# Summing both scan directions inside the forward units of a bidirectional Mamba kernel, against summing them in the output stage

## The chip, the cores and the metric

The kernel runs on one core of one Trainium2 chip. The metric is the device time of one execution in microseconds (us); lower is better. All data is float32.

## The reference, cut to what matters

An image of 1024 channels by 64 x 64 pixels is normalised, goes through a short decaying scan over channels and a token norm (stages that the change does not touch), and then through a bidirectional Mamba block over 4096 tokens:

```python
xz = (hidden @ in_proj_w.T).transpose(0, 2, 1)      # 2048 channels of x, 2048 of z
x, z = jnp.split(xz, 2, axis=1)
y_fwd = _direction(x, ...)                          # conv of 4 taps, projections, selective scan, 16 states
y_bwd = _direction(x[:, :, ::-1], ...)[:, ::-1, :]
y = (y_fwd + y_bwd) * silu(z.transpose(0, 2, 1))
out = nan_to_num(y @ out_proj_w.T)                  # then the residual is added
```

## The kernel before, in words

**Layout.** Tokens are cut into 8 chunks of 512 (`NCH`, `T`), the 2048 inner channels into 16 blocks of 128 (`DB`, `P`). A *unit* is one block of one chunk in one direction: 256 units (`NU`), first the 128 backward ones (chunks from the last to the first), then the 128 forward ones (`HALF` = 128). The kernel is a row of stages, with all engines joined between them; two matter here.

**`stage_scan`.** Every engine has its own program; semaphores join them. The order inside a unit is written out by hand over n = 0 to 15, the scan's states. For each n ScalarE (ACT) makes the decay `da` (L1026) and saves the end state of an earlier n (`save`, L1006); VectorE (DVE) scans (L1169) and, for 12 of the 16 states, multiplies with C (L1179, `weigh`); GpSimd (POOL) makes the scan's input `w` (L1120) and the products of the other four (L1129). TensorE (PE) adds all products of a unit up by transposing them one over the other into the bank `yT` (L893, L918, L926), so a unit's result is held by tokens, 128 tokens on partitions and 128 channels along the row. `yT_copy` (L987 to L992) moves it to `y_out` at n = 2 of the next unit, and the DMA queue of SyncE (SP) stores it (L742) to the scratch `yT` of its direction, one contiguous tile of 128 x 512 for each unit. The very last one is stored by L803.

PE also makes z: `in_step` in two halves at n = 0 and 2 of a forward unit, into the bank `in_ps`, which `in_copy` (L969 to L973) empties at n = 7 into `z_out`, two buffers; L768 stores it by channels to the scratch `z`, 2048 x 4096. Backward units make the next x the same way. The x projection of a chunk adds 16 blocks up in `proj_ps`, opened and closed by a matmul with zeros (`open_projection`, `close_projection`, L833 to L838). Before the units stand eight rounds of `before_scan`, on PE and ACT as a hardware loop (L936, L1079).

SP's program for a unit (L728 to L778) is in order: loads of the next-but-one unit's `wdt` and `xc`, the store of `y_out`, the broadcasts of B and C in the last unit of a chunk and the first of the next, the stores of `xc` and `z`, then at L770 a wait for **all** stores so far (`stored_to`), and behind it the loads of x, `wx` and `win` for later units.

**`stage_out`.** For each chunk 16 blocks are prepared and 8 groups of 128 output channels are made. To prepare a block, SP loads three tiles (L1263, L1265, L1267: forward y, backward y, z) into one of four slots, POOL adds the two y (L1293), PE transposes the sum in four 128 x 128 pieces (L1315), ACT makes silu(z) (L1303) and DVE multiplies the two into `yg` (L1343). A group is 16 float32 matmuls of 128 x 512 (L1325), which the profile shows as 32 (each is done in two passes), into one of two banks. DVE copies, cleans up and adds the residual (L1354 to L1366), SP stores. `chunks` (L1232) interleaves: at step q of chunk c an engine first prepares two blocks of chunk c + 1 and then does group q of chunk c; SP prepares one step ahead. Chunk 0 has nothing to hide behind. The eight 1 MB loads of `wout` stand on SP's queue behind chunk 0's tiles (L1268 to L1270), and chunk 1's first tiles behind them.

## Time and profile before

| what | us |
|---|---|
| median of 3 runs | 8527.85 (8518.41 to 8528.65) |
| the profiled execution, its own time | 8523.32 |
| its span, first to last instruction | 8521.3 |
| output stage, first DMA issue to the end of the span | 7484.4 to 8521.3, 1036.9 |
| PE busy, DVE busy, POOL busy, ACT busy | 7199.0, 7468.1, 6869.8, 4922.4 |

Times in rows are microseconds from the span's start. In a timeline row the first number is the start, the second the duration, then engine, line of the kernel, operation, and what it writes and reads; in brackets stands how long the engine had been idle and what ended the wait. PEld are weight loads of PE, SPq is SP issuing a DMA. A busy PE is not PE at its peak, since the ends of matmuls are modelled.

### The profile page before, as it was taken

How to read it: one execution, taken by the hardware profiler on the slowest of the kernel's cores; microseconds unless marked ns; L12 is line 12 of the kernel's file. 1: busy time of each engine (PE TensorE's matmuls, PEld its weight loads, DVE VectorE, ACT ScalarE, POOL GpSimd, SP SyncE). 2: the span in 40 equal slices, each digit the busy share in tenths (PEclk: the TensorE clock that was granted, in tenths of full speed). 3: DMA queues.
4: the chain of work that ended last, by engine and by line, in shares of the span. 5: the costliest groups of instructions: out<-in, count | busy, mean ns of one | idle time of the engine just before them, and what ended most of it. 6: DMA issues, size and time to landing. Idle time of an engine off the chain costs nothing. (4 is left out here: it accounts for less than half of the span.)

```text
span 8521.3 us, 107499 instructions
## 1 busy us (share of the span) xinstructions
PE 7199.0 (84%) x28624; PEld 4125.5 (48%) x28624; DVE 7468.1 (88%) x8300; ACT 4922.4 (58%) x11720; POOL 6869.8 (81%) x3058
## 2 busy tenths in 40 slices
PE   7568888888888888876888888888888887779999
PEld 3243554555555555544455545455554545434444
DVE  6922999999999999999999999999999999934443
ACT  3743666666666666666666666666666666610000
POOL 0613999999999999999999999999999999921110
PEclk9789999999999999977899999999999998889999
DMA  3273131323131323121223232323232322153442
GB/s 84 74 203 129 64 114 64 113 67 113 63 114 64 113 67 114 64 96 43 103 73 125 73 127 74 122 73 125 74 127 74 123 74 105 46 187 133 139 139 78
DMA packets 540787, 843.35 MB, mean 99 GB/s; under 512 B 112576, under 2 KB 260032, under 8 KB 522816
## 3 DMA queue, kind: packets, MB, share of 16 engines
q1 hardware_dynamic: 540224, 837.03, 29.6%
q8 instruction: 208, 3.41, 0.2%
q14 instruction: 355, 2.91, 0.1%
HBM read 583.83 MB, written 253.02 MB: 98 GB/s over the span
## 5 line engine op out<-in xcount | busy, mean ns | idle before, releaser
L1120 POOL TENSOR_TENSOR scan_w<-scan_du,scan_bcast_b 128x2048 f32<-128x2048 f32 x1023 | 4629.7, 4536 | 3.6 <-DMA scan_bcast_b<-bc 3.6
L1169 DVE TENSOR_TENSOR_SCAN scan_h<-scan_da,scan_state,scan_w 128x512 f32<-128x512 f32 x3072 | 3766.3, 1269 | 21.9 <-issue 14.5
L926 PE MATMUL scan_yT<-all_ident,scan_hc 128*128 128x128 f32 x12288 | 1991.5, 300 | 1010.1 <-DVE scan_hc L1179 994.7
L1026 ACT ACTIVATE scan_da<-scan_delta,scan_prm 128x512 f32<-128x512 f32 x4096 | 2802.9, 684 | 0.0
L926 PEld LDWEIGHTS scan_yT<-all_ident,scan_hc 128*128 128x128 f32 x12288 | 1464.0, 150 | 1975.6 <-DVE scan_hc L1179 1744.8
L1179 DVE TENSOR_TENSOR scan_hc<-scan_h,scan_bcast_c 128x512 f32<-128x512 f32 x3072 | 1935.4, 669 | 16.3 <-ACT scan_state L1006 16.3
L818 PE MATMUL scan_in_ps<-scan_hn,scan_win 128*128 128x512 f32 x3840 | 1737.1, 595 | 12.9 <-issue 12.9
L1006 ACT ACTIVATE scan_state<-scan_h 128x1 f32<-128x1 f32 x3072 | 518.2, 169 | 1756.7 <-DVE scan_h L1169 1755.1
L1129 POOL TENSOR_TENSOR scan_hp<-scan_hs,scan_bcast_c 128x512 f32<-128x512 f32 x1024 | 1306.3, 1276 | 71.9 <-issue 45.7
L1169 DVE TENSOR_TENSOR_SCAN scan_hs<-scan_da,scan_state,scan_w 128x512 f32<-128x512 f32 x1024 | 1283.9, 1254 | 27.8 <-ACT scan_da L1026 27.8
L818 PEld LDWEIGHTS scan_in_ps<-scan_hn,scan_win 128*128 128x128 f32 x3840 | 695.7, 191 | 719.3 <-issue 719.3
L1325 PE MATMUL out_o_ps<-out_yg,out_wout 128*128 128x512 f32 x2048 | 891.7, 594 | 0.0
L825 PE MATMUL scan_dt_ps<-scan_x,scan_diag 128*128 128x512 f32 x1920 | 883.6, 603 | 0.0
L1293 POOL TENSOR_TENSOR out_yf<-out_yf,out_yb 128x512 f32<-128x512 f32 x128 | 162.5, 1269 | 739.3 <-DMA out_z<-z 739.3
L893 PE MATMUL scan_yT<-all_ident,scan_hp 128*128 128x128 f32 x4096 | 715.0, 304 | 0.0
L1325 PEld LDWEIGHTS out_o_ps<-out_yg,out_wout 128*128 128x128 f32 x2048 | 386.3, 191 | 465.2 <-issue 465.2
L893 PEld LDWEIGHTS scan_yT<-all_ident,scan_hp 128*128 128x128 f32 x4096 | 562.7, 159 | 0.0
L1303 ACT ACTIVATE out_sz<-out_z 128x512 f32<-128x512 f32 x128 | 80.7, 630 | 820.6 <-DMA out_z<-z 820.6
L825 PEld LDWEIGHTS scan_dt_ps<-scan_x,scan_diag 128*128 128x128 f32 x1920 | 353.9, 195 | 357.9 <-issue 357.9
L1354 DVE COPY out_o<-out_o_ps 128x512 f32<-128x512 f32 x64 | 44.2, 691 | 522.3 <-PE out_o_ps L1325 316.7
L1006 ACT ACTIVATE scan_state<-scan_hs 128x1 f32<-128x1 f32 x1024 | 205.4, 201 | 319.0 <-DVE scan_hs L1169 317.9
L830 PE MATMUL scan_proj_ps<-scan_xc_out,scan_wx 128*96 128x512 f32 x512 | 383.0, 841 | 0.2
(126 smaller groups left out, 5517.9 us busy)
## 6 DMA issues: line engine op xcount, KB each, us to landing
yT<-scan_y_out SPq DMA_DIRECT2D x257, 256.0 KB, 2.0
scan_win<-winx SPq DMA_DIRECT2D x128, 512.0 KB, 3.5
xc<-scan_xc_out SPq DMA_DIRECT2D x256, 256.0 KB, 2.0
scan_xc<-xc SPq DMA_DIRECT2D x256, 256.0 KB, 3.5
scan_bcast_b<-bc SPq DMA_DIRECT2D x64, 1024.0 KB, 7.7
scan_bcast_c<-bc SPq DMA_DIRECT2D x64, 1024.0 KB, 8.1
scan_win<-winz SPq DMA_DIRECT2D x128, 512.0 KB, 4.7
scan_x<-x_pad SPq DMA_DIRECT2D x128, 257.5 KB, 2.6
```

The lines of the kernel that those rows point to most:

```text
L818: last = nc.tensor.matmul(bank, win[:, s, i], hn[:, i], start=(i == 0), stop=(i == KT - 1))
L825: last = nc.tensor.matmul(bank, diag[:, s, i], x[:, s, at:at + T], start=(i == 0), stop=(i == TAPS - 1))
L830: nc.tensor.matmul(proj_ps[0:XO, :], wx[:, s], xc_out[:, s], start=False, stop=False).then_inc(S["proj_mm"], 1)
L893: last = nc.tensor.matmul(yT[:, tb], hp[:, i, tb * P:(tb + 1) * P], ident[:], is_transpose=True, start=False, stop=False)
L926: last = nc.tensor.matmul(yT[:, tb], hc[:, i % NOUT, tb * P:(tb + 1) * P], ident[:], is_transpose=True, start=(i == 0 and tb == 0), stop=( ...
L1006: nc.scalar.activation(state_of(unit_, n_), h_slot(n_)[:, col:col + 1], ACT.Copy).then_inc(S["h_saved"], 1)
L1026: nc.scalar.activation(da[:, n % 2], delta[:, s], ACT.Exp, scale=decay(b, n)).then_inc(S["exp_done"], 1)
L1120: nc.gpsimd.tensor_tensor(w[:, g], du[:, s].unsqueeze(1).to_broadcast([P, G, T]), bcast_b[:, g * G:(g + 1) * G], ALU.mult).then_inc(S["w_d ...
L1129: nc.gpsimd.tensor_tensor(hp[:, i], hs[:, i], bcast_c[:, n], ALU.mult).then_inc(S["hp_done"], 1)
L1169: nc.vector.tensor_tensor_scan(flip(b, h_slot(n)), flip(b, da[:, n % 2]), flip(b, w[:, n // G, n % G]), state_of(b, n), ALU.mult, ALU.add) ...
L1179: nc.vector.tensor_tensor(hc[:, i % NOUT], h_slot(n), bcast_c[:, n], ALU.mult).then_inc(S["hc_done"], 1)
L1325: last = nc.tensor.matmul(o_ps[:, q % 2], wout[:, q, b], yg[:, g, b], start=(b == 0), stop=(b == DB - 1))
```

## The change

The backward units still store their y by tokens, now to one scratch `yT`. In a forward unit b the results of unit b - 1 and of its backward partner are summed: SP has loaded the partner's tile into the new buffer `y_back`, PE transposes `y_out` and `y_back` one over the other into the bank `in_ps` at n = 9 (`sum_y`, eight 128 x 128 transposes), ACT copies the bank to the new buffer `y_sum` at n = 14 (`y_copy`), and SP stores it by channels to the new scratch `y`. To make room `z_out` has one buffer instead of two. The output stage loads two tiles for a block instead of three and has no POOL sum and no transposes. Beside that, the matmuls with zeros around the projection are gone, and `before_scan` on PE is unrolled. The diff, cut to its core:

```diff
-        z_out = sc.sb("z_out", [P, 2, T])
-        zero = sc.sb("zero", [P, T])
+        z_out = sc.sb("z_out", [P, T])
+        y_back, y_sum = sc.sb("y_back", [P, TB, P]), sc.sb("y_sum", [P, T])
...
+        SKIP, DT_AT, SUM = 11, 13, 9
...
+            def load_y_back(b):
+                i = (2 * NCH - 1 - b // DB) * DB + b % DB
+                sp.dma_start(y_back[:], yT_d[i + 1]).then_inc(S["y_loaded"], LOAD)
+            def store_y(b):
+                hold(sp, S["y_copied"], b - HALF + 1, S["passed"])
+                sp.dma_start(y_d[ds(b % DB * P, P), ds(t0(b // DB), T)], y_sum[:]).then_inc(S["stored"], LOAD)
...
                 hold(sp, S["yT_copied"], b + 1, S["passed"])
-                sp.dma_start(yT_d[direction(b - 1)][(b - 1) % HALF + 1 if b else 0],
-                             y_out[:, (b + 1) % 2]).then_inc(S["stored"], LOAD)
+                if b <= HALF:
+                    sp.dma_start(yT_d[b], y_out[:, (b + 1) % 2]).then_inc(S["stored"], LOAD)
...
                 if not back(b):
                     hold(sp, S["in_copied"], b + 3, S["passed"])
-                    sp.dma_start(z_d[...], z_out[:, b % 2]).then_inc(S["stored"], LOAD)
+                    sp.dma_start(z_d[...], z_out[:]).then_inc(S["stored"], LOAD)
+                if b > HALF:
+                    store_y(b - 1)
+                if b >= HALF:
+                    load_y_back(b)
                 hold(sp, S["stored"], stored_to(b), S["passed"])
...
+            def sum_y(b):                                # PE
+                pe.wait_ge(S["yT_copied"], b + 2)
+                pe.wait_ge(S["in_copied"], b + 4 if b + 1 < NU else NU + 2)
+                for tb in range(TB):
+                    nc.tensor.matmul(in_ps[:, tb * P:(tb + 1) * P], y_out[:, b % 2, tb], ident[:],
+                                     is_transpose=True, start=(tb == 0), stop=False)
+                pe.wait_ge(S["y_loaded"], (b - HALF + 1) * LOAD)
+                for tb in range(TB):
+                    last = nc.tensor.matmul(in_ps[:, tb * P:(tb + 1) * P], y_back[:, tb], ident[:],
+                                            is_transpose=True, start=False, stop=(tb == TB - 1))
+                last.then_inc(S["y_mm"], 1)
...
+                    if n == SUM and b > HALF:            # PE, in unit b
+                        sum_y(b - 1)
...
-            open_projection()
-            with pe.Fori(0, DB // 2) as j:
+            for j in range(DB // 2):
                 before_scan(j)
-            close_projection()
...
+            def y_copy(b):                               # ACT
+                act.wait_ge(S["y_mm"], b - HALF + 1)
+                if b > HALF:
+                    act.wait_ge(S["stored"], stored_to(b))
+                nc.scalar.activation(y_sum[:], in_ps[:], ACT.Copy).then_inc(S["y_copied"], 1)
...
-                                act.wait_ge(S["stored"], stored_to(b - 2))     # before in_copy of z, n = 7
+                                act.wait_ge(S["stored"], stored_to(b - 1))
...
+                    if n == 14 and b > HALF:
+                        y_copy(b - 1)
...
             yT_copy(NU - 1)
+            y_copy(NU - 1)
```

and in `stage_out`:

```diff
-                    sp.dma_start(yf[:, i], yf_d[...]).then_inc(y_loaded[i], LOAD)
-                    sp.dma_start(yb[:, i], yb_d[...]).then_inc(y_loaded[i], LOAD)
+                    sp.dma_start(y[:, i], y_d[db * P:(db + 1) * P, ds(c * T, T)]).then_inc(y_loaded[i], LOAD)
                     sp.dma_start(z[:, i], z_d[db * P:(db + 1) * P, ds(c * T, T)]).then_inc(y_loaded[i], LOAD)
...
-                    nc.gpsimd.tensor_tensor(yf[:, i], yf[:, i], yb[:, i], ALU.add).then_inc(summed, 1)
...
-                    for tb in range(TB):
-                        last = nc.tensor.matmul(yt_ps[...], yf[...], ident[:], is_transpose=True, ...)
-            chunks(pe, prepare, project)
+            chunks(pe, lambda c, g, q: None, project)
...
-                    nc.vector.tensor_tensor(yg[:, g, u], yt_ps[:, s], sz[:, slot(q, s)], ALU.mult).then_inc(gated, 1)
+                    dve.wait_ge(y_loaded[slot(q, s)], y_loads(c, q))
+                    nc.vector.tensor_tensor(yg[:, g, u], y[:, slot(q, s)], sz[:, slot(q, s)], ALU.mult).then_inc(gated, 1)
```

## Rows read from the trace of the kernel before

**Rows 1.** The page's head: busy time of each engine.

```profile
PE 7199.0 (84%) x28624; PEld 4125.5 (48%) x28624; DVE 7468.1 (88%) x8300; ACT 4922.4 (58%) x11720; POOL 6869.8 (81%) x3058
```

**Rows 2.** Table by stretches, output stage: busy of each engine (instructions), clock, DMA share, GB/s.

```profile
7484.40:7550.80 66.40, 19.88 (x73) 13.10 (x74) 11.75 (x17) 12.76 (x20) 24.33 (x22) 0.50 0.97 362
7550.80:8511.90 961.10, 938.30 (x2489) 435.40 (x2488) 395.83 (x615) 69.02 (x110) 139.42 (x110) 1.00 0.37 124
...
7530.00:7540.00 10.00, 0.00 (x0) 0.00 (x0) 0.00 (x0) 0.00 (x0) 0.00 (x0) 0.50 1.02 428
```

**Rows 3.** Groups of instructions, forward units: busy us, mean ns, idle before, what ended it.

```profile
L1169 DVE TENSOR_TENSOR_SCAN scan_h<-scan_da,scan_state,scan_w 128x512 f32<-128x512 f32 x1544 | 1891.2, 1267 | 0.0
...
L1179 DVE TENSOR_TENSOR scan_hc<-scan_h,scan_bcast_c 128x512 f32<-128x512 f32 x1546 | 972.2, 667 | 0.0
...
L1169 DVE TENSOR_TENSOR_SCAN scan_hs<-scan_da,scan_state,scan_w 128x512 f32<-128x512 f32 x515 | 644.4, 1251 | 4.8 <-ACT scan_da L1026 4.7
...
L992 ACT ACTIVATE scan_y_out<-scan_yT 128x512 f32<-128x512 f32 x128 | 75.4, 589 | 0.7 <-PE scan_yT L926 0.7
```

**Rows 4.** Timeline of one forward unit, from 7349.49 to 7375.47.

```profile
7358.78 0.58 ACT L973 ACTIVATE scan_z_out<-scan_in_ps 128x512 f32<-128x512 f32 x1
...
7367.90 1.51 PE L926 MATMUL scan_yT<-all_ident,scan_hc 128*128 128x128 f32 x8 [3.03 <-DVE scan_hc L1179]
...
7369.74 0.69 ACT L1026 ACTIVATE scan_da<-scan_delta,scan_prm 128x512 f32<-128x512 f32 x1
...
7370.73 1.26 DVE L1179 TENSOR_TENSOR scan_hc<-scan_h,scan_bcast_c 128x512 f32<-128x512 f32 x2
7370.85 0.17 ACT L1006 ACTIVATE scan_state<-scan_h 128x1 f32<-128x1 f32 x1 [0.42 <-DVE scan_h L1169]
...
7371.92 2.44 DVE L1169 TENSOR_TENSOR_SCAN scan_h<-scan_da,scan_state,scan_w 128x512 f32<-128x512 f32 x2
```

**Rows 5.** Output stage, PE: transposes as a group, waits after 7550, the last nine groups.

```profile
L1315 PE MATMUL out_yt_ps<-all_ident,out_yf 128*128 128x128 f32 x512 | 84.5, 300 | 73.3 <-POOL out_yf L1293 73.3
...
PE out_yt_ps L1315 <- POOL out_yf L1293: 23.6, 29, 2.5
...
8388.33 123.62 PE out_o_ps L1325 x288
```

**Rows 6.** `wout` loads, landing; z's store and load, median us to landing; multiplies.

```profile
DMA to landing us min/median/max: 7.4/14.2/20.8
...
z<-scan_z_out SPq DMA_DIRECT2D x128, 256.0 KB, 2.3
...
out_z<-z SPq DMA_DIRECT2D x128, 256.0 KB, 4.4
...
L1343 DVE TENSOR_TENSOR out_yg<-out_yt_ps,out_sz 128x512 f32<-128x512 f32 x128 | 82.9, 683 | 64.4 <-PE out_yt_ps L1315 59.6 <-issue 4.8
```

**Rows 7.** Start of the output stage: silu of chunk 0's second and last block, `wout` issues.

```profile
7492.55 0.63 ACT L1303 ACTIVATE out_sz<-out_z 128x512 f32<-128x512 f32 x1 [2.59 <-DMA out_z<-z]
...
7519.52 4.58 SPq L1270 DMA_DIRECT2D out_wout<-wout  x8
...
7524.48 0.63 ACT L1303 ACTIVATE out_sz<-out_z 128x512 f32<-128x512 f32 x1 [2.21 <-DMA out_z<-z]
```

**Rows 8.** Timeline of PE, first dense matmuls of the scan stage after an idle PE.

```profile
572.21 15.98 PE L818 MATMUL scan_h<-scan_hn,scan_win 128*128 128x512 f32 x32 [13.22 <-DMA scan_win<-winx]
```

**Rows 9.** Timeline of the end of the scan stage.

```profile
7479.13 1.25 PE L926 MATMUL scan_yT<-all_ident,scan_hc 128*128 128x128 f32 x8 [0.87 <-DVE scan_hc L1179]
...
7480.47 0.60 ACT L992 ACTIVATE scan_y_out<-scan_yT 128x512 f32<-128x512 f32 x1 [4.75 <-PE scan_yT L926]
```

**Rows 10.** Timeline of SP and POOL where a forward chunk ends (unit start 7038.3).

```profile
7052.51 0.37 SPq L768 DMA_DIRECT2D z<-scan_z_out  x1
...
7069.09 0.83 SPq L695 DMA_DIRECT2D scan_bcast_c<-bc  x2
...
7078.34 1.28 POOL L1129 TENSOR_TENSOR scan_hp<-scan_hs,scan_bcast_c 128x512 f32<-128x512 f32 x1
```

More of the change, by code:

```diff
@@ L767, in unit @@
                     hold(sp, S["in_copied"], b + 3, S["passed"])
-                    sp.dma_start(z_d[ds(at * P, P), ds(t0(chunk), T)], z_out[:, b % 2]).then_inc(S["stored"], LOAD)
+                    sp.dma_start(z_d[ds(at * P, P), ds(t0(chunk), T)], z_out[:]).then_inc(S["stored"], LOAD)
+                if b > HALF:
+                    store_y(b - 1)
+                if b >= HALF:
+                    load_y_back(b)
                 hold(sp, S["stored"], stored_to(b), S["passed"])
@@ L801, in _ @@
                 unit(b)
-            hold(sp, S["yT_copied"], NU + 1, S["passed"])
-            sp.dma_start(yT_d[0][HALF], y_out[:, 1]).then_inc(S["stored"], LOAD)
+            store_y(NU - 1)
             hold(sp, S["stored"], stored_to(NU - 1) + LOAD, S["passed"])
@@ L827, in convolution, with project @@
                 last.then_inc(S["conv_mm"], 1)
[L829 to L838 removed]
+            def project(a):
+                nc.tensor.matmul(proj_ps[0:XO, :], wx[:, a % 2], xc_out[:, a % 2], start=(a % DB == 0),
+                                 stop=(a % DB == DB - 1)).then_inc(S["proj_mm"], 1)
+            def sum_y(b):
[9 more added lines that the diff above has]
+                last.then_inc(S["y_mm"], 1)
             def before_scan(j):
@@ L861, in in_step @@
                     pe.wait_ge(S["in_copied"], i + 2)
+                    if i > HALF + 1:
+                        pe.wait_ge(S["y_copied"], i - HALF - 1)
                     in_proj(i % 2, 0, KT // 2)
@@ L941, in _ @@
                 unit(b)
+            sum_y(NU - 1)
         @block.scalar
@@ L971, in in_copy @@
                 act.wait_ge(S["in_mm"], i + 1)
-                out = x[:, i % 2, 0:T] if back(i) else z_out[:, i % 2]
+                out = x[:, i % 2, 0:T] if back(i) else z_out[:]
                 nc.scalar.activation(out, in_ps[:], ACT.Copy).then_inc(S["in_copied"], 1)
@@ L980, in proj_copy @@
             def proj_copy(chunk):
-                act.wait_ge(S["proj_closed"], chunk + 1)
+                act.wait_ge(S["proj_mm"], (chunk + 1) * DB)
                 if chunk:
@@ L1081, in _ @@
             proj_copy(0)
[L1082 removed]
+            act.wait_ge(S["setup"], 3)
             dt_read(0)
@@ L1287, in _ @@
             nc.gpsimd.memset(minus[:], -1.0).then_inc(const_ready, 1)
-            def prepare(c, g, q):
-                for s in range(2):
-                    i = slot(q, s)
-                    pool.wait_ge(y_loaded[i], y_loads(c, q))
-                    nc.gpsimd.tensor_tensor(yf[:, i], yf[:, i], yb[:, i], ALU.add).then_inc(summed, 1)
-            chunks(pool, prepare, lambda c, g, q: None)
         @block.scalar
@@ L1308, in _ @@
         def _(pe):
-            def prepare(c, g, q):
-                for s in range(2):
-                    u = 2 * q + s
-                    pe.wait_ge(summed, c * DB + u + 1)
-                    pe.wait_ge(gated, c * DB + u + NY - 1)
-                    for tb in range(TB):
-                        last = nc.tensor.matmul(yt_ps[:, s, tb * P:(tb + 1) * P], yf[:, slot(q, s), tb * P:(tb + 1) * P],
-                                                ident[:], is_transpose=True, start=(tb == 0), stop=(tb == TB - 1))
-                    last.then_inc(yt_done, 1)
             def project(c, g, q):
@@ L1378, in metaformer @@
     bc = scratch("bc", (NCH, 2 * NS, T))
-    yT = [scratch(f"yT{d}", (NCH * DB + 1, P, TB, P)) for d in range(2)]
+    yT, y = scratch("yT", (NCH * DB + 1, P, TB, P)), scratch("y", (DI, HW))
     with Scope(nc, "all") as top:
@@ L1393, in metaformer @@
             stage_token_norm(nc, xn, ident, mv, hnT, x1T, x_pad)
-        stage_scan(nc, ident, hnT, winx, winz, wx, wdt, convp, par, skip, x_pad, xc, z, bc, yT)
-        stage_out(nc, passed, ident, yT[0], yT[1], z, wout, x1T, out)
+        stage_scan(nc, ident, hnT, winx, winz, wx, wdt, convp, par, skip, x_pad, xc, z, bc, yT, y)
+        stage_out(nc, passed, y, z, wout, x1T, out)
 def kernel(**inputs):
```

50 lines of the change are left out of this document (17 added, 33 removed).

## The prediction

> **What bounds the kernel now.** I read the busy times of the engines first [rows 1], then a table by stretches, because DVE is busy in one stage and PE in another [rows 2]. In the forward units the groups of instructions settle it: DVE's scans and products stand with 0.0, 0.0 and 4.8 us of idle time over 128 units [rows 3]. DVE sets the pace, 25.98 us for a unit [rows 4], so work added to another engine costs time only where DVE comes to wait for it, and then on each of 127 units.
>
> The output stage has two parts. From 7484.4 to 7550.8 PE has almost nothing to do, the granted clock is 0.50, the DMA engines are 97% busy: 66.4 us in which chunk 0 is prepared [rows 2]. From 7550.8 to 8511.9 PE is the bound: 961.1 us with 938.3 busy. Nine groups with nothing between them take 123.62 us, 13.74 each [rows 5]; 64 groups are 879.1 us, so 82.0 of the 961.1 are not dense matmuls. They are the transposes and what they bring: 23.6 us of waiting for POOL's sums, which themselves wait for tiles, and the rest the transposes (84.5 us busy over the stage, 512 of them, 448 of these for chunks 1 to 7) and some slow clock after waits [rows 5]. Behind the last group stand 9.4 us of DVE and the store, which the change leaves alone.
>
> **Part by part.**
>
> *Main part of the output stage.* The transposes go, and with them PE's wait for tiles, because PE's next wait is for all 16 multiplies of a chunk. Is DVE or a load late next? DVE has 395.8 us of work over 64 groups, 6.2 for each 13.74, the multiplies included [rows 2]; they now read SBUF instead of the bank, and I keep 0.68 us for each [rows 6]. SP issues the loads for step q + 2 when the result of group q is ready, about 6 us after its last matmul; four issues at up to 0.57 (eight took 4.58 [rows 7]), landing 4.4 [rows 6] and silu 0.63 make 13.3 us. DVE reaches those multiplies behind its work on group q + 1, at 13.74 + 6 = 19.7 us, so loads have 6 us in hand, where before PE's transposes asked for them at about 13.7 and had none. So: 64 x 13.74 = 879.1, and a slow start. PE now comes from full idleness. The scan stage shows that case: 32 passes after a 13.2 us pause took 15.98 us, 2.24 more than 13.74 [rows 8]. Sum 881.3, less than now by **79.8**. Bounds: no slow start, -2.2; up to 5 of waits that I do not see, +5.
>
> *Start of the output stage.* Chunk 0's second block came to silu at 7492.55 and its sixteenth at 7524.48: 2.28 us a block for three tiles, 786 KB, which is 345 GB/s with the DMA engines full [rows 2, 7]. Two tiles are 524 KB: 1.52 us a block at that rate, 1.22 at the 428 GB/s that the `wout` loads reach [rows 2]. Four slots also have a round trip, two issues 1.1, landing 4.4, silu 0.63 and multiply 0.68, 6.8 us or 1.7 a block. I take 1.6, between the two; the ends are 1.22 and 2.28 (nothing won). The second block comes 8.15 us after the stage's start now, and with 0.5 MB less ahead of it at 6.7; 14 x 1.6 later, at 29.1, the last. The first `wout` tile landed 7.4 after 7519.52, at 7526.9, 2.4 behind the last silu [rows 6, 7]; hence 31.5 now, and with the wait's end 32.0. Today PE also goes through chunk 1's first transposes before group 0, whose tiles stand behind 8 MB of `wout`; that wait is most of the 49.7 us (73.3 less 23.6) that PE waits here [rows 5]. DVE still prepares them before it reads group 0: 8.4 MB at 428 GB/s is 19.6 us, the tiles land at about 52, the bank is read at 54. PE needs it for its third group, at 32.0 + 15.98 + 13.74 = 61.7, so it is covered by 7.7 us. Gain 66.4 - 32.0 = **34.4**, with ends +5.3 (1.22) and -9.5 (2.28).
>
> The trace moves 428 GB/s in the `wout` stretch [rows 2]. The Trainium skill, "DMA: Bandwidth & Descriptors", section Specifications, gives a core about 358 GB/s of HBM. By it the 8.4 MB would take 23.4 us and still be covered; the trace exceeds it, and nothing above rests on it.
>
> *Forward units, PE.* Eight more transposes, 1.25 us at full clock [rows 9]. They stand at n = 9 behind the products of n = 7, where PE waits 3.03 us for DVE [rows 4]. Hidden; without that gap they would push later transposes, for which DVE has six `hc` buffers. What they wait for is old: `y_out` from n = 2, the bank from z's copy at n = 7, `y_back` loaded in the unit before.
>
> *Forward units, ACT.* One copy of 0.589 us [rows 3] behind `da` of n = 14. That one starts at 7369.74, ACT issues the next about 0.61 later, so the copy runs from 7370.35 to 7370.94; the save behind it is issued at 7370.85 today because it waits for DVE until then [rows 4]. The copy fits the wait to within 0.1 us. The product that needs the save is the second of the pair from 7370.73, at 7371.36, and the second scan of the pair from 7371.92, at 7373.1, needs the next `da`, over by 7371.7. Cost 0; upper end 0.1 us on each of 127 units, 13 us.
>
> *Forward units, SP and DMA.* One 256 KB store moved and one load added. SP now waits for the copy of n = 14, about 21.5 us into the unit, and for the landing of its store, 24 into it (z's lands in 2.3 [rows 6]); behind it are the loads of `win`, x, `wx`, then `wdt` and `xc`. All serve two units later, 20 us in hand. With one `z_out`, z's copy at n = 7 (9.3 into a unit, [rows 4]) needs the y store of the unit before landed: 11 us in hand. Where a chunk ends, the z store issued at 7052.51 lets SP on only at 7069, for it lands behind the broadcasts [rows 10]. The y store is issued at 7060 and lands a little behind; with `y_back`'s load ahead too, the last broadcasts of C are 1 to 1.5 us later. POOL uses the first at 7078.34, about 9 us after its issue [rows 10]; it may wait about 1 us there at 7 chunk ends, and DVE needs POOL's results only several us later. I put 0; upper end 7.
>
> *End of the scan stage.* Behind the last `yT_copy` (7480.47, 0.60) come eight transposes, 1.25 to 2.1 us (full or half clock), and a copy of 0.6 before the store [rows 9]: **+2.2** with the hops, bounds 2.0 and 2.9.
>
> *Zero matmuls, unrolling.* In the units they stand beside DVE's work. At the start, the closing one is 1 us ahead of the first `dt` matmul, but that waits for loads that SP issues later. 0, at best -1.
>
> **Sum** against the profiled execution: 8523.3 - 79.8 - 34.4 + 2.2 = 8411.3. The median of the runs lies 4.5 above the profiled execution, so I give 8413. A measurement of this kernel tells a change of 0.2%, 17 us, from none.
>
> **Rivals.**
>
> *The pace of DVE is touched.* The save or `da` behind the new copy comes late and DVE waits in each unit. For it: there is no more than 0.1 us between the copy's end and the save's present start. Against: 0.4 us to the product that needs it. At 0.2 us a unit 8438, at the full 0.59 8488. Chance 0.10.
>
> *Narrower rows of y make chunk 0 slow.* yT's tiles lie in one piece, y's rows are 16 KB apart. If y's tile costs as much as the two yT tiles, a block stays at 2.28 us and the stage starts 9.5 later: 8423. Against: z's tiles have the same spacing already. Chance 0.12. The Trainium skill, same page, section Latency and other measured facts, reports that DMA streams slow down where partitions' rows are a large power of two apart, 207 GB/s at 512 KiB, and would let one expect this; no run here shows that spacing.
>
> *Loads stay PE's bound in the main part.* DVE's multiplies wait for tiles and hand today's 23.6 us on: 8437. For it: SP's order is unchanged. Against: the 6 us above. Chance 0.06.
>
> *Slower than before.* `sum_y` comes late in each unit, ACT stands in front of its copy at n = 14, and `da` and DVE with it. PE passes n = 9 about 5.5 us before ACT asks, so lateness up to 5.5 costs nothing and any more goes straight into the unit. To lose the gain of 112 it must be late by 5.5 + 0.9 us in all 127 units; 7 us late is 1.5 x 127 = 190, 8602. PE has 3.03 us idle just before and the tile is loaded 15 us earlier. Chance 0.02.
>
> *It does not do what it says.* If the main part kept its 82 us for another reason (the matmuls themselves slower), only the start would gain: 8491. Chance 0.02.
>
> **How the numbers follow.** The forecast has 0.68. Its own range is 8400 (start at 1.22, no slow clock, low runs) to 8430. The rivals to 8438 bring the range up to 8440, which leaves out under 2 in 10: 8399 to 8440. Faster by over 0.2% in all but the fourth rival: 0.98, same 0.01, slower 0.01.
>
> **What the changed profile would show.** Right: DVE idle time in the forward units still a few us; PE's gap before the products of n = 9 shorter by 1.25; ACT's copy directly behind `da` of n = 14; the first `out_o_ps` matmul about 32 us after the stage's first DMA issue, silu 1.6 us apart; then 64 groups in about 881 us without PE waiting; the stage about 923 us long instead of 1037. Wrong: a wait of DVE on `da` or `h_saved` that repeats per unit, silu more than 2 us apart, gaps of PE between groups, or a granted clock below full in the last stage.

## The result and the profile after

| | before | changed |
|---|---|---|
| median of 4 runs, us | 8528.25 (8518.41 to 8528.82) | 8417.76 (8411.26 to 8419.72) |
| ratio to before, 95% | | 0.9872 (0.9855 to 0.9889) |
| profiled execution, us | 8523.3 | 8416.51 |
| span, us | 8521.3 | 8414.7 |

The kernel is faster by 1.28% by that ratio; the two medians of the table differ by 110 us. The forecast was 8413, its range 8399 to 8440.

The head of the page: busy time of each engine, and the costliest group of the output stage.

```profile
PE 7167.5 (85%) x29072; PEld 4105.6 (49%) x29072; DVE 7469.3 (89%) x8300; ACT 4976.0 (59%) x11848; POOL 6708.8 (80%) x2929
...
L1334 PE MATMUL out_o_ps<-out_yg,out_wout 128*128 128x512 f32 x2048 | 880.6, 593 | 36.5 <-DMA out_wout<-wout 36.5
```

The busy times hardly differ from [rows 1]: PE less by 32 us, POOL by 161, ACT more by 54. The gain of 107 us of span can't be read from them; it has to be read from the stages. I cut both traces at the same five instructions. The y_out copy is the one behind each scan unit (L992 before, L1013 after); the output stage starts with SP's first load and its main part with the first out_o_ps matmul. The figures below are differences of times in the timelines.

```
                                     before     after      difference
start to y_out copy of index 0       774.39     782.55       +8.16
backward half (index 0 to 128)      3377.33    3374.50       -2.83
forward half (index 128 to 256)     3328.75    3328.76       +0.01
last copy to first load of output      3.92       6.37       +2.45
start of the output stage             66.39      32.59      -33.80
its main part, to the last matmul    961.1      880.6       -80.5
tail                                   9.3        9.3        0
```

The two gains and the price at the end of the scan stage stand beside the sum's -34.4, -79.8 and +2.2. What the sum lacks is in the first two lines, +8.16 and -2.83; of it more below.

Table by stretches of the output stage (length, busy of PE, PEld, DVE, ACT and POOL with instructions, granted clock, DMA share, GB/s).

```profile
7492.00:7536.00 44.00, 11.23 (x23) 5.06 (x24) 11.07 (x16) 11.35 (x17) 1.45 (x3) 0.59 0.94 346
7536.00:8405.00 869.00, 869.00 (x2026) 384.56 (x2024) 391.30 (x616) 70.49 (x112) 0.00 (x0) 1.00 0.34 108
```

In the second line PE is busy for 869.00 of 869.00 us: not one wait is left where [rows 2] has 22.8 us of them. DVE's work hardly changed, and the DMA share fell from 0.37 to 0.34.

Timeline of the start of that stage: silu of chunk 0's second and last block, the `wout` loads, the first dense matmuls, silu of chunk 1's first block, and DVE's first read of a result.

```profile
7492.18 0.34 SPq L1293 DMA_DIRECT2D out_y<-y  x1
...
7497.85 0.63 ACT L1322 ACTIVATE out_sz<-out_z 128x512 f32<-128x512 f32 x1 [1.31 <-DMA out_z<-z]
...
7516.62 5.51 SPq L1297 DMA_DIRECT2D out_wout<-wout  x8
...
7522.02 0.63 ACT L1322 ACTIVATE out_sz<-out_z 128x512 f32<-128x512 f32 x1 [2.56 <-DMA out_z<-z]
...
7524.77 2.07 PE L1334 MATMUL out_o_ps<-out_yg,out_wout 128*128 128x512 f32 x2 [36.55 <-DMA out_wout<-wout]
...
7543.34 0.63 ACT L1322 ACTIVATE out_sz<-out_z 128x512 f32<-128x512 f32 x1 [20.68 <-DMA out_z<-z]
...
7545.96 0.68 DVE L1363 COPY out_o<-out_o_ps 128x512 f32<-128x512 f32 x1
```

Fourteen blocks between the two silus take 24.17 us, 1.73 each, where [rows 7] have 2.28. PE's first matmul waits for `wout` (36.55 us), no longer for a tile of y. It starts although chunk 1's tiles come only at 7543.34, and DVE reads the first bank 53.8 us into the stage.

A forward unit's end on ACT, DVE and SP, and PE around the new transposes in another unit.

```profile
7479.18 0.69 ACT L1054 ACTIVATE scan_da<-scan_delta,scan_prm 128x512 f32<-128x512 f32 x1
7479.79 0.59 ACT L1020 ACTIVATE scan_y_sum<-scan_in_ps 128x512 f32<-128x512 f32 x1
7480.08 1.35 DVE L1209 TENSOR_TENSOR scan_hc<-scan_h,scan_bcast_c 128x512 f32<-128x512 f32 x2
7480.29 0.17 ACT L1034 ACTIVATE scan_state<-scan_h 128x1 f32<-128x1 f32 x1
7480.35 0.69 ACT L1054 ACTIVATE scan_da<-scan_delta,scan_prm 128x512 f32<-128x512 f32 x1
...
7480.47 0.33 SPq L715 DMA_DIRECT2D y<-scan_y_sum  x1
```

```profile
4560.46 0.60 PE L851 MATMUL scan_in_ps<-all_ident,scan_y_out 128*128 128x128 f32 x4
4560.90 0.60 PE L855 MATMUL scan_in_ps<-all_ident,scan_y_back 128*128 128x128 f32 x4
4563.20 1.25 PE L946 MATMUL scan_yT<-all_ident,scan_hc 128*128 128x128 f32 x8 [1.71 <-DVE scan_hc L1209]
```

The copy stands behind `da`, and the save behind the copy follows without a wait, where [rows 4] have 0.42 us of one. PE still waits 1.71 us for DVE behind the eight transposes.

Waits of the forward half, the rows for DVE and POOL (total, times, longest).

```profile
DVE scan_hs L1199 <- ACT scan_da L1054: 4.5, 4, 1.5
POOL scan_hp L1160 <- DVE scan_hs L1199: 2.5, 1, 2.5
```

End of the scan stage: the last y_out copy, the transposes, the copy, the store.

```profile
7485.81 0.60 ACT L1013 ACTIVATE scan_y_out<-scan_yT 128x512 f32<-128x512 f32 x1 [4.77 <-PE scan_yT L946]
...
7486.46 0.91 PE L851 MATMUL scan_in_ps<-all_ident,scan_y_out 128*128 128x128 f32 x4 [0.77 <-ACT scan_y_out L1013]
...
7487.16 1.06 PE L855 MATMUL scan_in_ps<-all_ident,scan_y_back 128*128 128x128 f32 x4
7488.26 0.60 ACT L1020 ACTIVATE scan_y_sum<-scan_in_ps 128x512 f32<-128x512 f32 x1 [1.85 <-PE scan_in_ps L855]
7488.95 0.33 SPq L715 DMA_DIRECT2D y<-scan_y_sum  x1
```

### The profile page after: what moved, and what is told of

It reads as the page before. It is cut to its first block and busy times, and to the rows that moved or that the text cites. A ratio compares the mean times of both kernels' runs of the same rounds, so it can differ in the third digit from the quotient of the medians.

```text
span 8414.7 us, 108222 instructions
## 1 busy us (share of the span) xinstructions
PE 7167.5 (85%) x29072; PEld 4105.6 (49%) x29072; DVE 7469.3 (89%) x8300; ACT 4976.0 (59%) x11848; POOL 6708.8 (80%) x2929
## 3 DMA queue, kind: packets, MB, share of 16 engines
q1 hardware_dynamic: 540224, 837.03, 30.5%
q14 instruction: 345, 2.83, 0.1%
## 5 line engine op out<-in xcount | busy, mean ns | idle before, releaser
L1199 DVE TENSOR_TENSOR_SCAN scan_h<-scan_da,scan_state,scan_w 128x512 f32<-128x512 f32 x3072 | 3832.0, 1312 | 22.7 <-issue 15.3
L946 PE MATMUL scan_yT<-all_ident,scan_hc 128*128 128x128 f32 x12288 | 1969.7, 296 | 961.7 <-DVE scan_hc L1209 945.1
L946 PEld LDWEIGHTS scan_yT<-all_ident,scan_hc 128*128 128x128 f32 x12288 | 1423.5, 148 | 1965.8 <-DVE scan_hc L1209 1736.0
L1209 DVE TENSOR_TENSOR scan_hc<-scan_h,scan_bcast_c 128x512 f32<-128x512 f32 x3072 | 2000.1, 711 | 15.4 <-ACT scan_state L1034 15.4
L1199 DVE TENSOR_TENSOR_SCAN scan_hs<-scan_da,scan_state,scan_w 128x512 f32<-128x512 f32 x1024 | 1327.1, 1296 | 26.1 <-ACT scan_da L1054 26.1
L1334 PE MATMUL out_o_ps<-out_yg,out_wout 128*128 128x512 f32 x2048 | 880.6, 593 | 36.5 <-DMA out_wout<-wout 36.5
L911 PE MATMUL scan_yT<-all_ident,scan_hp 128*128 128x128 f32 x4096 | 694.3, 298 | 0.0
L911 PEld LDWEIGHTS scan_yT<-all_ident,scan_hp 128*128 128x128 f32 x4096 | 544.7, 155 | 0.0
L1128 POOL TENSOR_SCALAR scan_v<-scan_dt 128x512 f32<-128x512 f32 x256 | 156.9, 613 | 270.9 <-ACT scan_dt L968 250.7
```

The lines of the kernel that those rows point to most:

```text
L911: last = nc.tensor.matmul(yT[:, tb], hp[:, i, tb * P:(tb + 1) * P], ident[:], is_transpose=True, start=False, stop=False)
L946: last = nc.tensor.matmul(yT[:, tb], hc[:, i % NOUT, tb * P:(tb + 1) * P], ident[:], is_transpose=True, start=(i == 0 and tb == 0), stop=( ...
L1199: nc.vector.tensor_tensor_scan(flip(b, h_slot(n)), flip(b, da[:, n % 2]), flip(b, w[:, n // G, n % G]), state_of(b, n), ALU.mult, ALU.add) ...
L1209: nc.vector.tensor_tensor(hc[:, i % NOUT], h_slot(n), bcast_c[:, n], ALU.mult).then_inc(S["hc_done"], 1)
L1334: last = nc.tensor.matmul(o_ps[:, q % 2], wout[:, q, b], yg[:, g, b], start=(b == 0), stop=(b == DB - 1))
```

## Experiments: which part of the output stage brings what

The theory is that of the prediction: PE's transposes and the waits behind them cost the main part its 80 us; the start gains its 34 by a third fewer bytes, and because PE no longer goes through chunk 1's first transposes, whose tiles stand behind `wout`, before group 0. The first three kernels are the kernel before with parts of its output stage taken out; they compute no sum of both directions or no transposed one. The fourth has the new scan stage with the old output stage.

**Two loads, no transposes.** The new output stage alone. Edit to the kernel before:

```diff
-                    sp.dma_start(yb[:, i], yb_d[...]).then_inc(y_loaded[i], LOAD)
...
-                    nc.gpsimd.tensor_tensor(yf[:, i], yf[:, i], yb[:, i], ALU.add).then_inc(summed, 1)
...
-            chunks(pe, prepare, project)
+            chunks(pe, lambda c, g, q: None, project)
...
-                    nc.vector.tensor_tensor(yg[:, g, u], yt_ps[:, s], sz[...], ALU.mult).then_inc(gated, 1)
+                    nc.vector.tensor_tensor(yg[:, g, u], yf[:, slot(q, s)], sz[...], ALU.mult).then_inc(gated, 1)
```

> The kernel before with the new output stage alone: forward y (contiguous tiles) and z are loaded, nothing is summed or transposed (the backward y and the transposition are left out of the result). Theory (the whole gain is the output stage's, and the forward units' part costs only 2.4 us at the end of the scan stage): start about 32.6 us, main part about 880.5, total about 8528 - 34 - 80.5 = 8413.5, about 2.4 below the changed kernel, and chunk 0's blocks 1.7 us apart as there. Rival 1 (rows of y 16 KB apart load slower): blocks 1.5 us apart or less, start 3 us shorter than the changed kernel's. Rival 2 (the forward units lose time to the sum, 0.1 us each or more): 13 us or more below the changed kernel.

Measured: median 8422.87 (8411.68 to 8425.87), ratio 0.9869 (0.9853 to 0.9886). Start 32.9 us, main part 882.0, blocks 1.66 us apart. This is the changed kernel's time within the interval, so the whole gain lies in the output stage. (It is 9 us above what was expected; in its profile the first y_out copy comes 10.9 us later than before, at 785.30 instead of 774.39, in code that is the same.) And it answers the rival on y's rows: tiles in one piece come 1.66 us apart, rows 16 KB apart 1.73. That difference is no price of the rows. The same output stage behind the changed scan stage was profiled in five more kernels below, and there the blocks come 1.67 to 1.90 us apart and the start takes 32.6 to 35.6 us. What the runs exclude is the rival's 2.28.

**The sum kept, no transposes.** Three loads and POOL's addition stay; only PE's part goes, and DVE multiplies POOL's sum.

```diff
-            chunks(pe, prepare, project)
+            chunks(pe, lambda c, g, q: None, project)
...
-                    dve.wait_ge(yt_done, c * DB + u + 1)
+                    dve.wait_ge(summed, c * DB + u + 1)
```

> The kernel before with only PE's transposes of the output stage taken away: three tiles are still loaded and POOL still sums (the transposition is left out of the result). Theory (in the main part all 80 us are the transposes and the waits that they alone feel; at the start most of the gain is that PE no longer passes chunk 1's transposes, whose tiles stand behind wout, and only the rest is fewer bytes): main part 881, blocks of chunk 0 still 2.28 us apart, start about 43 instead of 66.4, total about 8528 - 80 - 23.5 = 8424.5. Rival (loads hold the main part too, and the start is a matter of bytes): the waits of 23.6 us stay somewhere, main part about 905, start 60 or more, total 8465 or more.

Measured: median 8417.16 (8416.71 to 8422.8), ratio 0.9869 (0.9852 to 0.9885). The PE group and silu of the second and the last block:

```profile
L1315 PE MATMUL out_o_ps<-out_yg,out_wout 128*128 128x512 f32 x2048 | 881.6, 593 | 43.3 <-DMA out_wout<-wout 43.3
```

```profile
7493.28 0.63 ACT L1303 ACTIVATE out_sz<-out_z 128x512 f32<-128x512 f32 x1 [2.29 <-DMA out_z<-z]
...
7521.69 0.63 ACT L1303 ACTIVATE out_sz<-out_z 128x512 f32<-128x512 f32 x1 [1.38 <-DMA out_z<-z]
```

The main part is as expected, 881.6 us. The start is not: 39.3 us instead of 66.4, and the blocks come 2.03 us apart, with the same three tiles each. So 2.28 was not what the bytes allow: 786 KB in 2.03 us is 387 GB/s against the 345 that I had read as the limit. What went is PE's step in the round trip of a slot (load, sum, transposes, multiply, load again): in the trace of before a block's transposes took 1.1 us at a clock of 0.50, and four blocks, one trip, took 9.1 us; here they take 8.1. That this step made the blocks slower is argued from two traces with it (2.28 here and 2.24 in the kernel with the new scan stage below) and one without; the steps from silu to silu show 1.94 to 2.84 us before, and 2.01 to 2.05 here, which is even enough to be the rate of the transfers. Twelve or so blocks of each kernel's start, the kernel before and then this one (clock, DMA share and GB/s at the end):

```profile
7488.00:7519.00 31.00, 14.17 (x52) 9.30 (x52) 8.30 (x12) 8.19 (x13) 16.46 (x13) 0.50 0.97 340
```

```profile
7488.00:7515.00 27.00, 0.00 (x0) 0.00 (x0) 7.71 (x12) 7.56 (x12) 15.16 (x12) 0.50 1.03 371
```

Of the 33.8 us that the change gains at the start, 27.1 come with all three loads in place. Some 3.5 of them (14 x 0.25) are the closer blocks. The other 23.6 lie between the last silu and the first dense matmul, 26.3 us before and 2.7 here: PE's wait for chunk 1's tiles and two transposes, which the next kernel shows. With the transposes gone, the third load and POOL's sum are thus worth the other 7 of the 34 us.

**Two loads, transposes kept.** The complement: the third load and POOL's addition go, PE transposes forward y alone.

```diff
-                    pe.wait_ge(summed, c * DB + u + 1)
+                    pe.wait_ge(y_loaded[slot(q, s)], y_loads(c, q))
```

> The kernel before without the backward tile and POOL's sum, but with the transposes (the backward y is left out of the result). Theory (a transposed pair of blocks costs PE 0.94 us, 14.67 less 13.74, and POOL's sum and the third load make the rest of the 80): main part 879 + 55 x 0.94 + up to 6 = 931 to 937, start about 55 because chunk 1's tiles still stand behind wout, total about 8528 - 27 - 11 = 8490. Rival (the waits come from the order of SP's loads and not from the third load and the sum): waits stay near 23.6, main part 957 or more, total 8513 or more.

Measured: median 8488.0 (8482.98 to 8490.97), ratio 0.9948 (0.9931 to 0.9965). The transposes as a group, and PE where the main part starts:

```profile
L1305 PE MATMUL out_yt_ps<-all_ident,out_yf 128*128 128x128 f32 x512 | 77.5, 296 | 39.6 <-DMA out_z<-z 39.6
```

```profile
7546.52 1.11 PE L1305 MATMUL out_yt_ps<-all_ident,out_yf 128*128 128x128 f32 x4 [20.89 <-DMA out_z<-z]
7547.88 1.11 PE L1305 MATMUL out_yt_ps<-all_ident,out_yf 128*128 128x128 f32 x4 [0.25 <-DMA out_z<-z]
7548.79 3.41 PE L1315 MATMUL out_o_ps<-out_yg,out_wout 128*128 128x512 f32 x4
```

Chunk 0 was ready at 7525, and PE waited another 20.9 us for chunk 1's first tiles, behind 8 MB of `wout`, only to transpose them before group 0. That is the second half of the old start: 54.6 us here, 11.8 less than before for the third load and POOL's sum. Blocks come 1.77 us apart, which is inside the spread of the kernels that have no transposes, so with two tiles the step of PE in the round trip does not show. The main part is 930.0: the transposes themselves cost 930.0 - 880.6 = 49 us in it, the waits that went with the third load and POOL 961.1 - 930.0 = 31. Both parts of the main part's gain are thereby measured, 49 + 31. The 31 need both causes: in the kernel before this one the third load and POOL's sum are still there, and without the transposes PE does not feel them.

**The new scan stage with the old output stage.** This kernel sums in the forward units and stores y by channels, but the output stage goes on as before, on a tensor of the old layout.

```diff
-        stage_out(nc, passed, y, z, wout, x1T, out)
+        stage_out(nc, passed, ident, yT, yT, z, wout, x1T, out)
```

> The changed scan stage with the output stage of before, which reads two tiles of yT and z, sums and transposes (the forward y is left out of the result). Theory (the forward units hide all of it, the end of the scan stage is 2.4 us longer): from the first to the last unit the same time as before within 1 us apart from stalls at chunk ends that both have, total 8530 to 8531. Rival (DVE comes to wait 0.1 us or more in each of 127 units): 8541 or more, or 8603 at the full 0.59 us.

Measured: median 8529.54 (8525.7 to 8542.95, 10 runs), ratio 1.0002 (0.9993 to 1.0012). Forward half 3328.39 us, an ordinary unit 25.98, start 65.4, main part 964.4. In an ordinary unit the store, the load, eight transposes and a copy cost nothing that can be measured. At chunk ends they do: POOL waits 0.8 to 1.1 us for the broadcast of C in four of the seven units that open a chunk, and in the unit behind each DVE waits for `da`:

```profile
DVE scan_hs L1199 <- ACT scan_da L1054: 2.6, 4, 0.9
```

Those four units take 26.6 to 27.0 us, 3 us together, and in the kernel before no unit at that place does. The half is still no longer than before, because none of this run's chunk ends meets the low clock that is described below, and one of the kernel before does.

## Experiments: how much room is left in the forward units

The prediction put the copy into a gap of ACT with some 0.1 us over, and the transposes into a gap of PE. Both were made larger.

**One and two more copies.** The bank is also copied to a spare tile, once or twice, in front of the copy that counts (the diff shows one).

```diff
+                    nc.scalar.activation(spare[:, r], in_ps[:], ACT.Copy)
                 nc.scalar.activation(y_sum[:], in_ps[:], ACT.Copy).then_inc(S["y_copied"], 1)
```

> The changed kernel with one more ACT copy of the bank (0.49 us from start to start, into a buffer that nothing reads) ahead of y_copy at n = 14 of each of 127 forward units. In the changed kernel the save behind y_copy ends 0.2 us before DVE's product that needs it. Theory (y_copy fits the wait and little is left): 0.5 - 0.2 = 0.3 us a unit, 38 us, total about 8456. Rival 1 (DVE already waits for it, so any more counts in full): 0.5 x 127 = 63 us, 8481. Rival 2 (ACT has much to spare there): 0, 8418.

> The same with two more copies. Theory: 1.0 - 0.2 = 0.8 us a unit, 102 us, total about 8520, and between one and two more copies the full 0.5 x 127 = 63. Rival 1: 127 us, 8545. Rival 2: under 60 us, under 8478.

Measured: one more, median 8462.6 (8458.31 to 8466.41), ratio 0.9915 (0.9899 to 0.9932), an ordinary unit 26.31 us; two more, 8532.51 (8524.78 to 8541.91), ratio 1.0001 (0.9991 to 1.0011), a unit 26.79. A wait that neither kernel has in its forward half appears, with one and with two copies:

```profile
DVE scan_hc L1212 <- ACT scan_state L1037: 28.8, 127, 0.2
```

```profile
DVE scan_hc L1212 <- ACT scan_state L1037: 90.0, 127, 0.7
```

The product waits for the save, in each of 127 units. The first extra copy costs 0.33 us, the second 0.48 more; 127 x 0.33 is 42 of the 45 us by which the median rose. From the start of one copy to that of the next are 0.48 us (the rows' 0.59 overlap), so the second counts in full and the copy of the change fitted with some 0.15 us over. Two extra copies eat the whole gain of the output stage. Their median is 12 us above what was expected, and 13 us of slow chunk ends stand in their profile. The rival on DVE's pace was near in mechanism, though it did not happen.

**Twice the transposes.** y_out is transposed three times into the bank, 16 transposes for 8; the bank then holds forward y three times.

```diff
-                for tb in range(TB):
-                    nc.tensor.matmul(in_ps[...], y_out[:, b % 2, tb], ident[:], is_transpose=True, ...)
+                for r in range(3):
+                    for tb in range(TB):
+                        nc.tensor.matmul(in_ps[...], y_out[:, b % 2, tb], ident[:], is_transpose=True, ...)
```

> The changed kernel with 16 transposes in sum_y instead of 8 (y_out is added three times over, so the sum is another one). Theory (they stand in a gap of PE of 3 us and y_copy comes 5 us later): no change in the forward units, about 1.3 to 2 us more at the end of the scan stage, total 8418 to 8421. Rival (PE's part is on DVE's path): 1.25 us or more in each unit, 8575.

Measured: median 8438.73 (8433.67 to 8442.93), ratio 0.9889 (0.9873 to 0.9906). Neither expectation holds. Ordinary units take 25.98 us, as the theory said, but the time rose by 21. The steps between y_out copies show where: those at the ends of the seven inner chunks take 27.6 to 29.3 us, in the changed kernel 26.0 at five of them and 27.6 at two. The forward half is 16.3 us longer; the rest of the 21 lies in stages that the edit does not touch. PE and what it delays, at such an end:

```profile
4546.58 1.90 PE L947 MATMUL scan_yT<-all_ident,scan_hc 128*128 128x128 f32 x8 [1.86 <-DVE scan_hc L1210]
4548.41 2.07 PE L826 MATMUL scan_dt_ps<-scan_proj,scan_wdt 64*128 64x512 f32 x2
4550.41 5.23 PE L831 MATMUL scan_in_ps<-scan_hn,scan_win 128*128 128x512 f32 x8
```

```profile
4560.05 0.60 ACT L993 ACTIVATE scan_z_out<-scan_in_ps 128x512 f32<-128x512 f32 x1 [3.85 <-PE scan_in_ps L831]
...
4561.93 1.28 DVE L1200 TENSOR_TENSOR_SCAN scan_hs<-scan_da,scan_state,scan_w 128x512 f32<-128x512 f32 x1 [2.99 <-ACT scan_da L1055]
```

The granted clock has fallen to half there: two dt matmuls take 2.07 us and half of in_proj 5.23 (1.12 and 3.70 in the changed kernel). The clock is low from 4546.7 to 4553.5; in the changed kernel it is low from 4537.6 to 4541.0, on work with nobody waiting. z's bank is late, ACT stands before its copy, `da` behind ACT, DVE behind `da`. Theory now: it is not the added PE time that costs, but the place in the unit to which it moves the low clock. Two runs tested it, by leaving the extra transposes out of some units.

**Three sums of a chunk spared** (the last two blocks of a chunk and the first).

```diff
-                for r in range(3):
+                for r in range(1 if b % DB in (0, DB - 2, DB - 1) else 3):
```

> The eight extra transposes of c2_twice_the_transposes stay in 13 of a chunk's 16 units; those for the sums of the last two blocks of a chunk and of the first are taken out. In c2 the ordinary units kept their 25.98 us and the units at chunk ends took 27.6 to 29.3. Theory (what the extra transposes cost is only where the granted clock falls at a chunk's end: pushed from before n = 9's products to the dt matmul and in_proj, so that z's bank is late): the chunk-end units are back at 26.0 to 27.6 as in the changed kernel, the middle of the forward half (block 128 to 256) is within 4 us of the changed kernel's 3328.8, and the median is 8418 to 8424. Rival (PE's total work in the half makes the ends slow, wherever it stands): the half stays some 16 us above the changed kernel's, median about 8437.

Measured: median 8437.32 (8434.79 to 8438.53), ratio 0.9891 (0.9875 to 0.9908); the forward half is still 16.9 us longer. By itself this looks like the rival. But the trace shows that the clock falls at 4545.7 again, and that the last extras before it, those of the chunk's 14th block at 4535, had not been spared: the edit came one unit too late to tell. So:

**One sum of a chunk spared**, that of the 14th block.

```diff
-                for r in range(3):
+                for r in range(1 if b % DB == DB - 3 else 3):
```

> As c2_twice_the_transposes, but one unit in each chunk of 16 goes without the eight extra transposes: that of the sum of the chunk's 14th block, which runs one unit ahead of the low clock. In c4_twice_but_chunk_ends, which spared the three sums after it, PE still came out of shorter pauses there, its clock stayed full at 4536 to 4545 and was 0.50 to 0.62 at 4545 to 4551, on the dt matmul and in_proj of z. Theory (it matters where in the unit the clock falls): with this unit's sum as in the changed kernel the clock falls at its products of n = 9 again (near 4537) and is full when in_proj starts; the chunk-end units are 26.0 to 27.6, the forward half is within 4 us of 3328.8, median 8418 to 8424. Rival (the sum of PE's work over many units decides): 14 of 16 units still have the extras, the half stays some 16 us longer, median about 8437.

Measured: median 8423.83 (8419.67 to 8425.24), ratio 0.9872 (0.9856 to 0.9889); the forward half is 3.5 us longer than the changed kernel's. Two stretches ahead of a chunk's end, first of the kernel with all extras, then of this one (clock in the third column from the right):

```profile
4536.00:4545.00 9.00, 6.89 (x51) 5.27 (x49) 9.00 (x11) 4.57 (x14) 9.00 (x3) 1.00 0.33 106
4545.00:4551.00 6.00, 4.42 (x11) 2.50 (x12) 6.00 (x7) 5.16 (x15) 5.24 (x2) 0.64 0.75 217
```

```profile
4536.00:4545.00 9.00, 6.57 (x35) 4.92 (x36) 9.00 (x12) 5.37 (x16) 9.00 (x4) 0.81 0.45 114
4545.00:4551.00 6.00, 6.00 (x23) 3.11 (x24) 6.00 (x7) 4.17 (x13) 3.88 (x3) 1.00 0.62 183
```

With one unit of 16 changed, the low clock is back in the first stretch, in_proj finds it full, five of the seven chunk ends take 26.0 us, and 13 of the 16.3 us are gone. The 15 units of a chunk that keep their extras cost next to nothing (the expectation's 14 was a miscount). Of the 3.5 us that are left, 1.7 are one end at 29.3 where the changed kernel has one at 27.6, and most of the rest are two units behind a chunk's first, where DVE waits 1.2 and 0.5 us for `da` as in the kernel with the new scan stage alone.

All twelve profiles bear it out, also those with no extra transposes. Each has seven inner chunk ends. The table tells apart whether the clock was low during the first half of z's in_proj there (which then takes 4.8 to 6.5 us instead of 3.70), and by how much the unit is longer than an ordinary one of the same kernel:

```
                                          ends with low clock      each costs    the other ends
before                                          1 of 7               3.36          0.0 to 0.4
its scan stage in the first three tests     3, 1 and 1 of 7       1.66 to 3.36     0.0 to 0.4
changed                                         2 of 7               1.66          0.0
its scan stage, old output / eight slots     0 and 2 of 7         1.66 to 3.36     0.0
one / two more copies                        3 and 5 of 7         1.64 to 3.37     0.0 to 0.3
twice the transposes / three sums spared     7 and 7 of 7         1.63 to 3.36      none
one sum spared                                  2 of 7            1.66 to 3.36     0.0
```

Of 84 ends the 34 with the low clock on in_proj all cost 1.6 to 3.4 us, and none of the 50 others costs more than 0.4. The theory holds: the slowdown comes from where the clock falls. The kernel before has the same stall at one of its ends. What decides where the clock falls stays open.

## Experiment: eight slots for the tiles

If the start is bound by the slots' round trip and not by bytes, more slots should shorten it. The changed kernel with eight slots, and the first `wout` tile issued ahead of the last loads:

```diff
-        NY = 4
+        NY = 8
...
-            return q % 2 * 2 + s
+            return q % 4 * 2 + s
...
+                if isinstance(c, int) and c == 0 and q == KT // 2:
+                    sp.dma_start(wout[:, 0], wout_d[0]).then_inc(w_loaded[0], LOAD)
```

> The changed kernel with eight slots for y, z and silu(z) in the output stage instead of four, and the first wout tile loaded halfway through chunk 0. Theory (chunk 0's blocks come 1.73 us apart because four slots go round in 6.9 us, not because the bytes take so long; the run with three tiles and no transposes moved 786 KB in 2.03 us, 387 GB/s): blocks 1.3 to 1.4 apart, first matmul of group 0 about 26 to 27 us after the stage's start instead of 32.6, total 8411 to 8412. Rival (bytes bound it at the 303 GB/s of the changed kernel): blocks stay 1.7 apart, only the 1.3 us that PE waited for wout behind the last multiply go, start about 31.

Measured: median 8419.99 (8413.1 to 8421.18), ratio 0.9865 (0.9848 to 0.9881). Start 30.5 us, near the rival's 31, but not by its mechanism. PE's first matmul now waits for the last multiply:

```profile
L1336 PE MATMUL out_o_ps<-out_yg,out_wout 128*128 128x512 f32 x2048 | 880.7, 593 | 34.4 <-DVE out_yg L1354 34.4
```

Blocks come 1.51 us apart up to the tenth and 1.36 behind the `wout` tile, 524 KB in each, which is 347 and 385 GB/s. The step with the tile in it takes 3.89 us, 2.5 more than its neighbours, which is most of what the start lacks to the 26 to 27 us expected. So the slots did bind a little: 1.51 lies below the 1.66 to 1.90 of all seven profiles with four slots, two tiles and no transposes. Ten of the 13 steps without the tile are 1.34 to 1.41 us, 391 to 372 GB/s, close to the 387 of the kernel with three tiles and no transposes, so there the transfers are the likely bound. The 2 us are not told from the changed kernel by the medians; no version here beats it.

## Why the prediction was right

**Main part.** Predicted 881.3, measured 880.6. The term of 64 groups at 13.74 us, 879.1, holds (13.73 from group to group), the slow start costs 1.5 us (the first group takes 15.26) where 2.2 were put, and DVE and the loads do not take the place of the wait removed: PE is busy without a gap. The kernel with two loads and the transposes shows 49 us for the transposes and 31 for what came with the third load and POOL's sum.

**Start.** Predicted 32.0, measured 32.6, but by a reading of which one part fell. The terms were 6.7 us to the second block, 14 blocks at 1.6, and `wout` with the wait's end 2.9 us behind the last silu. Measured: 5.7, 14 at 1.73, and 2.75: together +0.6 (-1.0, +1.8 and -0.2). What failed is the step that took 2.28 us a block for the rate of full DMA engines; the kernel without transposes moves the same bytes at 2.03, and two tiles at that rate would be 1.35. The round trip of the slots, the estimate's other term with 1.7 us, was the better one of the two, and 1.6, taken between a wrong bound and a right one, came as near as it did partly by luck. That the start came within 0.6 us is luck too: the five other kernels with the same output stage start at 32.6 to 35.6 us. One reading of the trace of before was wrong and not used in the sum: PE's wait for chunk 1's tiles is not most of the 49.7 us but 21 of them, the rest being waits for chunk 0's blocks.

```profile
7547.84 1.11 PE L1315 MATMUL out_yt_ps<-all_ident,out_yf 128*128 128x128 f32 x4 [20.87 <-POOL out_yf L1293]
```

Chunk 1's tiles still came late, but nobody needed them sooner: DVE read the first bank at 53.8 us, predicted 54.

**Forward units.** Predicted 0. An ordinary unit takes 25.98 us before and after, and the scan stage's part alone has a ratio of 1.0002. That the half differs by only 0.01 us is luck: before has one chunk end that costs 3.36 us at the low clock, the changed kernel two that cost 1.66 each. Over kernels with the same scan stage the half varies from 3328.75 to 3331.65 (before's) and from 3328.39 to 3330.60 (the changed one's). The room for the copy was put at 0.1 us to the save's place of before and 0.4 to the product; it is about 0.15. PE's gap in front of the products shrank as said, to 1.7 to 2.1 us. At the chunk ends POOL waits 3.2 us in 3 waits for the broadcast of C, against 1.2 in one: less than the 1 us at each of 7 ends that was allowed. It reaches DVE once, with 0.3 us (a unit of 26.38); in the kernel with the new scan stage alone it costs some 3 us, within the upper end of 7.

**End of the scan stage.** +2.45 against +2.2 with bounds of 2.0 and 2.9; the transposes ran at the low clock. In the kernel with the new scan stage alone it is +1.8, with eight slots +2.7.

**What the sum lacks** is about 5 us: it gave 8411.3 for the profiled execution, which took 8416.51. The first y_out copy comes 8.2 us later than before, and 7.8 of these are there at the first matmul of the scan stage (579.97 instead of 572.21), ahead of all that was changed. In three kernels with exactly the old stages up to the output stage, that copy came at 775.52, 782.97 and 785.30 against 774.39. It is a spread between programs or executions in the first stages; whose is open, since no run was made for it. The backward half gives 2.8 of it back. The forecast of 8413 is also not quite what its own sum says: 8411.3 and the 4.5 us between the median and the profiled execution of before are 8415.8. The measured median is 8417.76.

**The rivals.** DVE's pace: not touched in ordinary units, with 0.15 us to spare. Rows of y: refuted by the first experiment. The Trainium skill, "DMA: Bandwidth & Descriptors", section Latency and other measured facts, reports slow streams at far larger spacings; at 16 KB no cost is seen here beyond the spread between profiles (1.67 to 1.90 us a block, against 1.66 in one piece), and larger spacings no run here shows. Loads as the bound of the main part: no gap of PE. A late sum: PE reaches it early, and even 16 transposes leave an ordinary unit at 25.98. The mechanism that could have cost some 20 us, a low clock that moves onto in_proj at a chunk's end, was in none of them, although the trace of before shows it once.

## What to carry to other kernels

An operation moved off the bound engine into gaps of another stage is worth its own time there and also the waits it dragged along: here 49 us of transposes were accompanied by 31 us of waits in the main part and by most of the 34 at the start. Before calling a stretch bound by bytes because the DMA share is near 1, count the round trip of its buffers, with every step of it at the clock that it really has. And where work fits into a gap, ask not only for how long: doubling it cost next to nothing in 15 units of 16 and 1.6 to 3.4 us where it moved the low clock onto a matmul that others wait for. And before an equal total is read as no effect, compare the single steps: here two different sets of stalls gave the same sum.

## What was not expected of the hardware

- Eight more transposes in a unit moved the fall of the granted clock from 4537.6 to 4546.7, about 9 us later. In the changed kernel it begins behind a wait of 2.13 us, and in the other behind waits of 1.26, 0.57 and 1.86 us; what decides between them stays open.
- A DMA share of 0.97 stood beside 340 GB/s while chunk 0 came in, and the same tiles came at 371 GB/s (share 1.03) once the transposes were gone. The share says that the engines have something in hand, not that no more would fit.
- DVE's rows in the forward half are longer after than before (the scans of h 1315 ns on average against 1267, the products 715 against 667) at the same 25.98 us a unit and without idle time. The durations of back-to-back rows overlap: DVE's 28 rows of one unit add up to 28.2 us before and 29.0 after, more than the unit. So the period of a unit is the measure, not their mean.
